# A graph network's score stage: who carries TensorE's signals, the last matmul or a drain behind it

## What is computed

```python
h = jnp.maximum(_layernorm(x, axis=-1), 0.0)
gl = (h @ W_l).reshape(n, H, F_OUT)                 # H = 6, F_OUT = 64
gr = (h @ W_r).reshape(n, H, F_OUT)
s = jax.nn.leaky_relu(gl[src] + gr[dst], 0.2)       # one row an edge
e = jnp.einsum('ehf,hf->eh', s, att)                # its six scores
m = jax.ops.segment_max(e, dst, num_segments=n)
p = jnp.exp(e - m[dst])
alpha = p / (jax.ops.segment_sum(p, dst, num_segments=n)[dst] + 1e-16)
out = jax.ops.segment_sum(alpha[:, :, None] * gl[src], dst, num_segments=n)
x = x + jax.nn.selu(out.mean(axis=1) + bias)
```

## Time and profile before

| | us |
|---|---|
| timed runs, median of 3 | 4990.21 |
| lowest and highest | 4989.92, 4996.32 |
| profiled execution, span | 5820.0 |
| profiled execution, other time | none is shown |
| score stage in it (3736 to 5058) | 1322 |

### The profile page before, as it was taken

The page is one execution under the profiler, slowest core; times in us unless marked ns, Lnnn a source line. Parts: engine busy times, 40 slices in busy tenths (PEclk is TensorE's granted clock), DMA queues, the critical chain, the costliest instruction groups (busy, mean ns, idle before and its releaser), DMA issues. The chain is left out here.

```text
span 5820.0 us, 104938 instructions
## 1 busy us (share of the span) xinstructions
PE 4388.1 (75%) x29528; PEld 2834.6 (49%) x29528; DVE 4126.9 (71%) x7954; ACT 2011.5 (35%) x6556; POOL 3270.2 (56%) x2950
## 2 busy tenths in 40 slices
PE   2999899989677777756777777376777667549998
PEld 1444444444344444445555555244444434349998
DVE  4767676766777676767777777466666666789998
ACT  2656566666000000134434444000000000057775
POOL 4666666663566666455555554455555555325554
PEclk6999999999788888778888888688888888779998
DMA  4333333331212111121111111233333333211111
GB/s 114 91 90 94 87 87 93 94 87 48 52 43 44 40 43 44 23 47 45 45 42 47 44 45 35 63 101 103 100 103 101 105 106 102 78 43 47 49 49 33
DMA packets 493105, 394.00 MB, mean 68 GB/s; under 512 B 346007, under 2 KB 379168, under 8 KB 492904
## 3 DMA queue, kind: packets, MB, share of 16 engines
q1 hardware_dynamic: 395496, 303.53, 18.3%
q0 software_dynamic: 90560, 83.37, 8.0%
q10 hardware_dynamic: 6976, 6.23, 0.3%
HBM read 355.34 MB, written 37.42 MB: 67 GB/s over the span
## 5 line engine op out<-in xcount | busy, mean ns | idle before, releaser
L1093 POOL DMA_INDIRECT edge_src_rows<-table_wh,edge_gather_idx x806 | 867.8, 1077 | 503.0 <-issue 229.7
L950 POOL DMA_INDIRECT edge3a_src_rows<-table_h,edge3a_gather_idx x808 | 763.1, 944 | 632.7 <-issue 259.0
L2165 PE MATMUL edge3a_z_ps<-Wz,edge3a_both_ends_t 128*128 128x396 f32 x1616 | 736.3, 600 | 405.0 <-DVE edge3a_terms L2258 322.0
L1123 PE MATMUL edge_sums_ps<-edge_onehot_src,edge_halves 128*128 128x512 bf16 x4840 | 890.0, 331 | 43.2 <-issue 32.4
L950 POOL DMA_INDIRECT table_cat<-table_hn,table_gather_idx x592 | 624.9, 1056 | 479.6 <-PE edge_sums_ps L1795 181.2
L1508 POOL DMA_INDIRECT edge_src_rows<-table_h,edge_gather_idx x608 | 609.1, 1002 | 424.4 <-issue 175.4
L2258 DVE SCALAR_TENSOR_TENSOR edge3a_terms<-edge3a_z_ps,att_z 128x792 f32<-128x792 f32 x404 | 386.1, 977 | 486.6 <-DMA edge_edge_attr<-in_ea 307.5
L2165 PEld LDWEIGHTS edge3a_z_ps<-Wz,edge3a_both_ends_t 128*128 128x128 f32 x1616 | 346.6, 226 | 733.7 <-DVE edge3a_terms L2258 368.3
L1123 PEld LDWEIGHTS edge_sums_ps<-edge_onehot_src,edge_halves 128*128 128x128 f16 x4840 | 385.6, 97 | 477.4 <-issue 69.5
L2577 PE MATMUL edge3b_sums_ps<-edge3b_onehot,edge3b_weighted 128*128 128x128 f32 x4848 | 572.9, 279 | 6.3 <-DVE layers_accT L2615 4.4
L2577 PEld LDWEIGHTS edge3b_sums_ps<-edge3b_onehot,edge3b_weighted 128*128 128x128 f32 x4848 | 553.6, 193 | 12.0 <-DVE layers_accT L2615 4.6
(11 more groups left out here) (370 smaller groups left out, 7950.6 us busy)
## 6 DMA issues: line engine op xcount, KB each, us to landing
edge_dst_row<-in_dst_row SPq DMA_DIRECT2D x102, 512.0 KB
edge3a_dst_row<-in_dst_row SPq DMA_DIRECT2D x102, 512.0 KB
edge_window<-table_wh_parts SPq DMA_DIRECT2D x816, 48.8 KB
edge3a_window<-table_h SPq DMA_DIRECT2D x816, 32.0 KB
edge_edge_attr<-in_ea SPq DMA_DIRECT2D x101, 256.0 KB
kept_rows<-edge3a_src_rows SPq DMA_DIRECT2D x101, 256.0 KB
edge3b_src_rows<-kept_rows SPq DMA_DIRECT2D x101, 256.0 KB
edge_edge_attr<-in_ea SPq DMA_DIRECT2D x101, 128.0 KB
```

The lines of the kernel that those rows point to most:

```text
L950: nc.gpsimd.indirect_dma_start(self.slot(b, j), None, self.table[:, :], bass.IndirectOffsetOnAxis(ap=self.idx[b][:, j:j + 1], axis=0)).the ...
L1093: nc.gpsimd.indirect_dma_start(g[q][:, j, :], None, k.t_wh[:, :], bass.IndirectOffsetOnAxis(ap=idx[q][:, j:j + 1], axis=0)).then_inc(gathe ...
L1123: mm = pe.matmul(acc[:, i, 0:w], halves[q][:, j, a, :, :].rearrange("p h d -> p (h d)"), hot[:, o:o + w], start=first and a == 0, stop=False)
L2165: mm = pe.matmul(zp[q % 2][:, i, 0:H * ZH], hcT[h][:, j * P:(j + 1) * P], k.Wz[:, :], start=True, stop=True)
```

## The change

The three places where PE's last matmul of a group carried a semaphore increment (in `turn`, `project` and `turn_scores`) now issue the matmul without it and then a drain, an instruction of PE's sequencer, which carries the increment. Order and number of all other instructions on all engines stay as they are; lines from L2174 on move down by one.

```diff
                     for j in range(B):
                         cols = slice(j * P, (j + 1) * P)
                         pe.matmul(hcTp[D:P, cols], win[h][:, j, :], oht[h][:, cols], start=True, stop=True)
-                        mm = pe.matmul(hcTp[0:D, cols], g[b][:, j, :], k.ident[:, :], start=True, stop=True)
-                    mm.then_inc(hcTp_ready, 1)
+                        pe.matmul(hcTp[0:D, cols], g[b][:, j, :], k.ident[:, :], start=True, stop=True)
+                    pe.drain().then_inc(hcTp_ready, 1)

                 def project(n, h, q):

                     pe.wait_ge(terms_ready, 4 * (n - 1) + q + 1)
                     for i in (0, 1):
                         j = 2 * q + i
-                        mm = pe.matmul(zp[q % 2][:, i, 0:H * ZH], hcT[h][:, j * P:(j + 1) * P],
+                        pe.matmul(zp[q % 2][:, i, 0:H * ZH], hcT[h][:, j * P:(j + 1) * P],
                                        k.Wz[:, :], start=True, stop=True)
-                    mm.then_inc(z_ready, 1)
+                    pe.drain().then_inc(z_ready, 1)

                 def turn_scores(n, h):
                     pe.wait_ge(scT_ready, n)
                     pe.wait_ge(summed, 2 * n + 4)
                     pe.matmul(scTp[:, :], scs[h][:, :, :].rearrange("p h b -> p (h b)"), k.ident[:, :],
-                              start=True, stop=True).then_inc(scTp_ready, 1)
+                              start=True, stop=True)
+                    pe.drain().then_inc(scTp_ready, 1)
```

## The result

The changed kernel takes 5032.69 us (median of 4 runs, 5030.54 to 5035.85) beside 4991.67 for the kernel before on the same chip (4 runs, 4989.92 to 4996.32): a ratio of 1.0082, 95% interval 1.0068 to 1.0097, 41 us slower. The forecast was slower by 70.

A forecast was written before the change was run, and what follows sets the result against it. POOL's gathers bound the score stage at 10.0 us a batch; drains add 2.9 to PE's 7.7, making 10.6 to 10.7, so (10.7 - 10.0) x 101 = 71: 4990 + 70 = 5060 us, range 4980 to 5200.

The forecast's parts named there:

- The hold: Score stage: matmul signals due during POOL's gathers come only after the train; taken as added by the profiled execution.
- Rival 2: Each batch's handover to ACT and DVE: hold is in timed runs, drain's signal passes it; 4750, at most half, 4870; 0.10.
- Rival 3: PE in the score stage: drain is held and stops the sequencer; 150 us on top of 70, 5210 us; chance 0.09.
- POOL's round of 10.0: Score stage, timed run: POOL's 8 gathers at 1.25 us are the slowest loop, 10.0 us a batch.
- Rival 4: Score stage: POOL is faster without the profiler, 7.6 us a batch, so DVE's 8.43 is the base; 5220 us; chance 0.09.
- Rival 1: Score stage: PE's round stays under POOL's timed round, so the drains stay hidden; no change, 4990 us; chance 0.20.
- The sum on PE: PE in the score stage: six drains add 2.9 us a batch, taking its round from 7.7 to 10.6 to 10.7 us.
- the allowance of 0.05 us behind the matmul's end: Each PE drain: taken to end 0.05 us behind the end of the last matmul.
- The 7.7: PE's round before the change: 8.65 us a batch less 0.95 of wait for DVE.
- the bounds: Drains' cost on PE: 1.4 us a batch, round 9.1, no change; up to 3.7, round 11.4, +141 us.
- ACT, DVE, SP and buffers at no cost: Engines and buffer reuse gated by PE's signals: all have slack in a round of 10.7 us, costed at nothing.
- The last batches: Score stage's end, without gathers: 10.7 us a batch instead of 8.65; under 10.0 would point to rival 1.

The follow-up runs named there:

- the later one of before: The kernel before, unchanged, profiled and timed once more: span 4993.6 us, timed median 4994.31 us, ratio 1.0003 to before.
- drains that carry nothing: Against the changed kernel, signals put back on the matmuls, with a drain that signals nothing behind each of the six groups: 5023.95 us, ratio 1.0065.
- the four z drains: Kernel before with six of eight gathers a batch and only the four z pairs' signals on drains: 4959.39 us, ratio 0.9933.

## Why the prediction was right, and where a size was off

**The hold.** Right. Taken for something that the profiled execution added, it was found neither in the change's profile nor in the later one of before, and both spans fit their timed runs. Rival 2 (the hold in the timed runs, the drain's signal passes it) had nothing to gain. Rival 3 expected drains held for many us and a span well over 5820; the span is 5034.1, the median drain 1593 ns. Both fall for these executions. What a drain does in an execution with the hold was not seen: none of the later ones had it.

**POOL's round of 10.0 as the base.** Right: 10.02. Rival 4 (0.30 us between gathers as the profiler's doing, base 8.43) would have needed a before at 4832; that time only came with two gathers taken away.

**Rival 1, hidden under POOL.** It holds for up to four drains and fails at five. Its general form, that the change hides, fell by 0.35 to 0.43 us a batch only (10.35 in the round shown, 10.43 in the mean of the loop, for 10.0): with a PE round shorter by that much it would have held.

**The sum on PE.** Here a size was off. "Sum: 1.56 + 0.52 + 0.51 + 0.32 = 2.9 us a batch" measured 2.65, the round 10.35 where 10.6 to 10.7 was forecast, so that (10.7 - 10.0) x 101 = 71 became (10.37 - 10.02) x 101 = 35. The timed runs' 41 has an interval of 34 to 48 us, which holds that. By terms, each from the start of a group's last matmul to the start of the next group's first; a group's last matmul starts one matmul (0.50, or 0.27 in the turnings) before the end that its row gives:

| to | forecast | measured | from the rows of the change |
|---|---|---|---|
| second, fourth pair | 0.75 each | 0.71 each | 3701.34 - (3699.53 + 1.59 - 0.50) = 0.72; 0.71 with three digits |
| turning | 0.95 | 0.90 | 3703.34 - (3701.34 + 1.59 - 0.50) = 0.91 |
| score turning | 0.62 | 0.50 | 3705.53 - 3705.04 = 0.49 |
| third pair | 0.52 | 0.49 | 3706.16 - (3705.53 + 0.41 - 0.27) = 0.49 |
| next first pair | 0.85 | 0.82; 1.20 every fourth time | 3709.88 - (3707.97 + 1.59 - 0.50) = 0.82; 3699.53 - (3697.24 + 1.59 - 0.50) = 1.20 |

More than half of the gap is the allowance of 0.05 us behind the matmul's end, which came out at 0.02 (3702.959 - 3702.938; 0.020 to 0.028 for nearly all drains of the stage) and counts six times. The other large one is the score turning, where "0.1 from weight load to matmul" did not occur (the records show 0.007). One term was left out and works the other way: the end of the loop's pass on PE's sequencer, 0.38 us every fourth batch. It was hidden under matmuls before and stands in the open behind a drain. With it the loop's mean round is 10.43. That two errors of opposite sign met is luck, if a small one. The experiments give the same sizes by another way: the four z drains 9.67 - 7.7 = 1.97 (forecast 4 x 0.52 = 2.08), the turning's 10.12 - 9.67 = 0.45 (0.51), the score turning's 10.37 - 10.12 = 0.25 (0.32). The 7.7 in the first is the prediction's sum from rows and no measured round, and the first holds the loop's 0.10 as well. A sum of 2.65 against 2.9 is a good estimate of a part, but the time is the difference of two nearly equal rounds, and there an error of 0.3 us a batch is half of the result. That is why the bounds were +0 to +141.

By the latency of a lone matmul that the Trainium skill gives (TensorE: Matmul & The Clock Gate, Single matmul latency), the estimate was 1.05 us a batch. Measured were 2.65, and some 2.7 with the loop's end. By the records of the change from 3250 to 4190 us the sequencer spends 1.48 us a batch between the ends of its drains and the weight loads that follow, on its own small instructions and the issue of the load. That is a little over half. What the rest, some 1.25, is made of the traces don't split. It isn't far from that estimate.

**ACT, DVE, SP and buffers at no cost.** Right, as far as the traces show. The 0.08 us a batch by which the change is slower than drains that carry nothing lie in PE's own gaps, 13 to 16 ns at each of the six, and not in a wait for another engine. They are part of the 2.65. Why PE loses that much more when the drain carries the increment stays open.

**The last batches.** Forecast at 10.7 without gathers. The last gather of the change starts at 4227.7, and ACT's starts behind it are these:

```profile
4237.11 1.02 ACT L2205 ACTIVATE edge3a_both_ends_t<-edge3a_both_ends_t_ps 128x1024 f32<-128x1024 f32 x1 [9.20 <-PEq L2158]
4247.35 1.02 ACT L2205 ACTIVATE edge3a_both_ends_t<-edge3a_both_ends_t_ps 128x1024 f32<-128x1024 f32 x1 [9.07 <-PEq L2158]
4257.26 1.02 ACT L2205 ACTIVATE edge3a_both_ends_t<-edge3a_both_ends_t_ps 128x1024 f32<-128x1024 f32 x1 [8.73 <-PEq L2158]
```

10.24 and 9.91 us, for 8.65 in the earlier trace rows. The 10.24 is what one round in four takes in the loop too. The very last is under the 10.0 that the text named as the mark of rival 1, and yet the loop runs at 10.43. It is not a round of the loop: the last batches are written out behind it with fixed numbers to wait for, so PE's sequencer has less to compute. At three of its six drains the next weight load follows 0.053 us behind the drain's end, where the loop has 0.186. So it was a poor mark for the loop, and too near to the bound.

## What to carry to other kernels

A stop of an in-order sequencer costs what it had issued ahead: here 0.25 to 0.5 us a drain, a little over half of it its own small instructions and weight loads, however short the drain itself. Count the loop's own counter and branch among them. How much of that shows is decided by the round of the slowest engine: add the stops to PE's round and subtract the other engine's, and expect a threshold. Before a sum is made against a profile, compare its span with the timed runs; where they differ by a sixth, as here, say which wait is the difference, and if a second execution can be had, take it first.

## What the runs showed of the hardware that I had not expected

- The hold of the earlier trace rows, matmul signals that come out only behind a train of gathers, was in one profiled execution and in none of the eleven others of this kernel and its variants, all with the same gathers or six of eight. It added 830 us to that one. What brought it on stays open; no other run provoked it.
- More stops, yet a warmer clock. PE's granted clock over the score stage is 0.99 with the change and 0.95 before it (the windows above), so it stays at 2.4 GHz through stops of 0.2 to 0.4 us every 2 us or so, from 3225.5 us to the stage's end. In the later execution of before it falls to 1.2 GHz 22 times between 3230 and 4225 us, each time during a wait of PE for gathers, of 1.95 to 4.96 us, or within 1.4 us behind it. Most waits of about 2 us bring no fall. Behind one that did, a turning matmul goes from 0.29 to 0.42 us:

```profile
4214.80 0.29 PE L2156 MATMUL edge3a_both_ends_t_ps<-edge3a_onehot_t,edge3a_window 128*64 128x128 f32 x1 [3.48 <-DMA edge3a_src_rows<-table_h,edge3a_gather_idx]
...
4215.28 0.42 PE L2157 MATMUL edge3a_both_ends_t_ps<-ident,edge3a_src_rows 128*64 128x128 f32 x1
```

PE's busy time in the stage is longer all the same (888 for 834 us), because matmuls that ran into each other now stand apart.
- The drain ends within some 0.02 us of the modelled end of the last matmul, and a second one on an empty array costs under 0.1.
